# Attention with its VectorE queue reordered, the copy of O moved from ScalarE to VectorE, and V products two key tiles later

## What is computed

```python
x = x + attention(layernorm(x))
x = x + ffn(layernorm(x))
# attention, per sequence b and head h
q, k = rope(q), rope(k)                       # first 32 of 64 dimensions
sim  = einsum('bhid,bhjd->bhij', q, k) * 64 ** -0.5
attn = softmax(sim, axis=-1)
out  = einsum('bhij,bhjd->bhid', attn, v)     # heads joined, then @ Wout + bout
# ffn: gelu((x @ U1) @ V1 + b1) @ U2 @ V2 + b2
```

## Time and profile before

| | |
|---|---|
| median of 3 runs | 1569.16 us (1568.19 to 1571.64) |
| the profiled execution | 1572.87 us, its span 1570.9 us |
| PE busy | 1443.6 us, 92% of the span |
| ACT, POOL, DVE busy | 68%, 63%, 60% |
| chain that ended last | PE 73%, issue 8%, ACT 7%, POOL 5%, DVE 5% |

### The profile page before, as it was taken

One profiled execution on the slowest core, in us unless ns is written; L12 is line 12 of the kernel. 1 busy time (PEld: TensorE's weight loads), 2 busy tenths in 40 slices (PEclk: granted clock), 3 DMA queues, 4 the chain that ended last, 5 costly groups with the idle time before them and its releaser, 6 DMA issues.

```text
span 1570.9 us, 29110 instructions
## 1 busy us (share of the span) xinstructions
PE 1443.6 (92%) x7289; PEld 541.1 (34%) x7289; DVE 942.3 (60%) x1809; ACT 1063.3 (68%) x2024; POOL 988.6 (63%) x517
## 2 busy tenths in 40 slices
PE   3698999999999999999999999999999999998886
PEld 1133333333324333333424333332433333343323
DVE  7465665566565656656566566656665665657444
ACT  2476776677767677767767776767767676776564
POOL 4389856658485665748476575848566574848631
PEclk9699999999999999999999999999999999999999
DMA  5412131221303122220313122130312222031002
GB/s 149 86 31 54 33 80 23 57 58 38 77 14 79 27 60 51 56 59 14 79 36 75 27 57 58 26 80 24 79 23 59 56 52 63 14 79 37 1 15 67
DMA packets 76421, 80.76 MB, mean 51 GB/s; under 512 B 29252, under 2 KB 43080, under 8 KB 76072
## 3 DMA queue, kind: packets, MB, share of 16 engines
q1 hardware_dynamic: 74880, 78.89, 21.5%
q10 hardware_dynamic: 1448, 1.00, 0.3%
HBM read 22.56 MB, written 2.36 MB: 16 GB/s over the span
## 4 chain that ended last, share of the span: by engine, by line
PE 73%; issue 8%; ACT 7%; POOL 5%; DVE 5%; ACTq 1%; DMA 1%; SPq 0%; DVEq 0%; POOLq 0%
PE O L399 26%; PE S L387 13%; PE S L388 11%; PE MD L408 10%; PE TILE L319 4%; PE TILE L337 4%; PE TILE L313 3%; PE TILE L329 2%; ACT OS L504 2%; ACT PF L532 2%; ACT LEFT L517 2%; POOL SA L706 2%; DVE STAGE L556 1%; ACT STAGE L443 1%; POOL WRAW L299 1%
## 5 line engine op out<-in xcount | busy, mean ns | idle before, releaser
L706 POOL TENSOR_TENSOR SA<-PF 128x1024 f32<-128x1024 f32 x256 | 623.0, 2442 | 434.6 <-DVE SUM L633 292.2
L625 DVE CUSTOM_DVE_ANT_0 LEFT<-MR,LEFT 128x512 f32<-128x512 f32 x512 | 353.3, 690 | 481.8 <-ACT LEFT L517 477.1
L532 ACT ACTIVATE PF<-S 128x512 f32<-128x512 f32 x1024 | 553.1, 596 | 44.7 <-PE S L388 35.2
L517 ACT ACTIVATE LEFT<-MD 128x512 f32<-128x512 f32 x512 | 308.3, 602 | 381.8 <-PE MR L409 349.2
L399 PE MATMUL O<-PF,V 128*64 128x512 f32 x2048 | 502.7, 612 | 15.2 <-ACT OS L504 15.2
L387 PE MATMUL S<-QK 128*128 128x512 f16 x1024 | 393.2, 384 | 10.5 <-ACT PF L532 10.5
L388 PE MATMUL S<-QK 128*128 128x512 f16 x1024 | 389.2, 380 | 0.0
L408 PE MATMUL MD<-KD,QK 64*128 64x512 f16 x512 | 225.5, 440 | 15.8 <-ACT LEFT L517 9.1
L636 DVE TENSOR_TENSOR SUM<-SUM,SA 128x1024 f32<-128x1024 f32 x128 | 227.0, 1773 | 8.6 <-POOL SA L706 8.3
L409 PE MATMUL MR<-QK 64*128 64x512 f16 x512 | 225.8, 441 | 0.0
L399 PEld LDWEIGHTS O<-PF,V 128*64 128x64 f32 x2048 | 125.6, 137 | 225.4 <-issue 158.8
(11 more groups left out here) (101 smaller groups left out, 1001.3 us busy)
## 6 DMA issues: line engine op xcount, KB each, us to landing
QK<-STAGE SPq DMA_DIRECT2D x128, 256.0 KB, 3.2
QK<-STAGE SPq DMA_DIRECT2D x128, 128.0 KB, 3.1
RB<-den SPq DMA_DIRECT2D x128, 128.0 KB, 3.0
KD<-KDS SPq DMA_DIRECT2D x128, 32.0 KB, 2.7
X<-in_L_attn_queries SPq DMA_DIRECT2D x4, 512.0 KB, 12.9
RT<-DS SPq DMA_DIRECT2D x128, 2.0 KB, 1.7
out<-X SPq DMA_DIRECT2D x8, 256.0 KB, 2.3
WRAW<-in_L_attn_Wkv SPq DMA_DIRECT2D x1, 1024.0 KB, 8.9
```

The costliest lines, as they stand in the source:

```text
L517: e.activation(LEFT[:, side, :], MD[:, :], ACT.Relu).then_inc(left_over, 1)
L532: e.activation(PF[:, t % SLOTS, z * HALF:(z + 1) * HALF], S[:, bank_of(t, z), :], ACT.Exp, scale=EXP_SCALE).then_inc(exped, 1)
L625: e.tensor_tensor_reduce(LEFT[:, side, :], MR[side][:, :], LEFT[:, side, :], 1.0, LOWEST, ALU.add, ALU.max, MX[:, place % 2, q:q + 1]).the ...
L706: e.tensor_tensor(SA[:, (t // 2) % 2, :], PF[:, t % SLOTS, :], PF[:, t % SLOTS + 1, :], ALU.add).then_inc(two_summed, 1)
```

## The change

1. `dve_step` does the tile work of its own step: in odd steps before `dve_max`, in even steps behind it. Statistics, invert, sums and norm now stand behind both.
2. The copy of O goes from ACT (`kt` = 2) to DVE (`dve_copy_out`), first in the step `kt` = PV_LAG - 2 = 4.
3. `PV_LAG` is 6: V products come two steps later, a head's first at `kt` = 6.
4. Tiles move: q's second rot tile from step 11 to 12, its pass tile from 13 to 14, V tiles and output tiles of the earlier pair of heads two steps later, DOWN tiles of the last iteration too.
5. The 12 units ahead of the loop alternate between MD and S[2], and each waits for the last but one.

```diff
-PV_LAG = 4
+PV_LAG = 6
-QK_AT = (1, 3, 4, 7, 8, 10, 11, 13)
+QK_AT = (1, 3, 4, 7, 8, 10, 12, 14)
-V_AT = {14: (1, 0), 16: (1, 1), 22: (0, 0), 24: (0, 1)}
+V_AT = {16: (1, 0), 18: (1, 1), 22: (0, 0), 24: (0, 1)}
-OUT_AT = {17: (1, 0), 19: (1, 1), 28: (0, 0), 30: (0, 1)}
+OUT_AT = {19: (1, 0), 21: (1, 1), 28: (0, 0), 30: (0, 1)}
-DOWN_AT = (12, 18, 21, 22, 23, 24)
+DOWN_AT = (12, 14, 17, 23, 25, 26)
+        LESS = [MD[:, :], S[:, 2, :]]
 # act_step
-            if kt == 2 and (not it.first or h > 0):
-                act_copy_out(e, it.i * GH + h - 1, (h - 1) % GH)
 # dve_tiles
-            for n, kind, args in it.at(t - 1):
+            for n, kind, args in it.at(t):
+        def dve_copy_out(e, head, h):
+            rows = slice(DH * (h % 2), DH * (h % 2) + DH)
+            e.wait_ge(pv_done, KT * (head + 1))
+            wait(e, added, head - h % 2 - 2)
+            for z in range(2):
+                cp = e.tensor_copy(OS[rows, h // 2, z, :], O[DH * z:DH * z + DH, :])
+            cp.then_inc(o_copied, 1)
 # dve_step
-            dve_tiles(e, it, t)
+            if kt == PV_LAG - 2 and (not it.first or h > 0):
+                dve_copy_out(e, it.i * GH + h - 1, (h - 1) % GH)
+            if t % 2 == 1:
+                dve_tiles(e, it, t)
+            if not (it.last and u >= STEPS):
+                dve_max(e, it.step(u), it.i * GH + u // KT, (u // KT) % GH, u % KT, u % 2)
+            if t % 2 == 0:
+                dve_tiles(e, it, t)
             ... (statistics, invert, sums, norm as before)
-            if not (it.last and u >= STEPS):
-                dve_max(e, it.step(u), it.i * GH + u // KT, (u // KT) % GH, u % KT, u % 2)
 # ahead of the loop, PE (ACT likewise)
-                pe_unit(pe, u, u // KT, u % KT, u % 2)
+                wait(pe, left_over, u - 1)
+                pe_unit(pe, u, u // KT, u % KT, u % 2, LESS[u % 2])
 # behind the loop
-            act_copy_out(act, GROUPS * GH - 1, GH - 1)
+            dve_copy_out(dve, GROUPS * GH - 1, GH - 1)    # behind the last two dve_sum
```

More of the change, by code:

```diff
@@ L402, in pe_values, with pe_unit @@
             mm.then_inc(pv_done, 1)
-        def pe_unit(e, u, place, q, side):
-            wait(e, left_over, u)
+        def pe_unit(e, u, place, q, side, less):
             wait(e, max_read, u - 1)
-            e.matmul(MD[:, :], QHH[0:DH, place, q:N:KT], KD[:, place, :], start=True, stop=True)
+            e.matmul(less, QHH[0:DH, place, q:N:KT], KD[:, place, :], start=True, stop=True)
             e.matmul(MR[side][:, :], QHH[DH:P, place, q:N:KT], KMH[DH:P, place, 512:N],
@@ L416, in pe_next_unit @@
                 e.wait_ge(handed[place], HAND * (it.i + u // STEPS + 1))
-            pe_unit(e, it.step(u), place, q, u % 2)
+            e.wait_ge(left_over, it.step(u))
+            pe_unit(e, it.step(u), place, q, u % 2, MD[:, :])
         def pe_step(e, it, t):
@@ L496, in act_tiles @@
                     act_rot(e, args, it.i + 1)
[L498 to L505, removed]
         def act_max(e, head, place):
@@ L511, in act_max, with act_left @@
             e.activation(MN[:, place % 2, :], MX[:, place % 2, :], ACT.Copy, scale=-1.0 / MSCALE).then_inc(max_found, 1)
-        def act_left(e, u, side):
+        def act_left(e, u, side, less):
             e.wait_ge(unit_made, u + 1)
             wait(e, max_read, u - 1)
-            e.activation(LEFT[:, side, :], MD[:, :], ACT.Relu).then_inc(left_over, 1)
+            e.activation(LEFT[:, side, :], less, ACT.Relu).then_inc(left_over, 1)
         def act_step(e, it, t):
@@ L525, in act_step @@
             if t % 2 == 0 and more:
-                act_left(e, it.step(t + LEAD), t % 2)
+                act_left(e, it.step(t + LEAD), t % 2, MD[:, :])
             for z in range(2):
@@ L902, in _ @@
             for u in range(LEAD):
-                act_left(act, u, u % 2)
+                act_left(act, u, u % 2, LESS[u % 2])
                 if u == KT + 1:
```

## The result

The changed kernel takes **1605.07 us** (median of 4 runs, 1604.58 to 1607.7) against 1568.68 us for the kernel before on the same chip: a ratio of 1.0235 (1.0213 to 1.0258). It is 36 us slower. The forecast was 1582, slower by 13.

What follows compares the result with a forecast made beforehand. TensorE's work (92% of the span) plus its queue's gaps bounds the kernel. New gaps less 3.6 us make +1.3 an iteration, times 15 +19.5, less 2.4, 1.9 and 2.3: +13, so 1582 us; own range 1573 to 1600.

Steps and rivals of the forecast that it cites:

- copies of O at the other three heads: VectorE's copies end 2.2 to 3.3 us behind the V pair, TensorE wants O after 3.2 to 4.5: no gap.
- gap of step 15: TensorE's unit of step 16 waits for LEFT behind GpSimd's late rot_add: 1.1 us (0.6 to 1.6).
- last iteration: It makes no q and k and only sheds copies: 2.3 us saved.
- Step 1: Loses 0.95 us as ScalarE comes back late from the loop's end; nothing in the change alters that.
- Removed, 3.6 us an iteration: TensorE's gaps for O and tiles at steps 3, 4, 11 and 27, with small gaps, go: 3.6 us.
- chain from the sum to the unit of step 12: Sum at kt = 7 starts at +4.14, rot_add ends at +14.8, 3.3 us later; TensorE's gap at step 11 is 2.0 us.
- Copy of O at step 13: VectorE's copy follows maximum and sum; O is free at +19.8, wanted at +19.1: 0.6 us gap.
- Rival (c): Worse case, chance 0.06: stretched kt = 3 sums make copies late at steps 5 and 29, later gaps larger: 1613 us.
- The hand-over, 1.2: Transfers of q and k for the next iteration land at +40.2, TensorE wants them at +39.0: 1.2 us gap.
- The prologue, -2.4, and the tail, -1.9: Two banks save 2.4 us over the twelve units before the loop; last scores come 1.9 us earlier, gained at the tail.
- Rival (a): Faster case, chance 0.30: GpSimd not late; 1517 us with only the copy's 0.6 gap, 1547 with only step 11's.
- The lock: VectorE with two SBUF inputs and GpSimd exclude each other; copies of O out of PSUM cost GpSimd nothing, else up to 1.3 us.

Runs made afterwards that it cites:

- Run 1: The changed kernel with part 0 of the sum (kt = 7) first in its step on VectorE again, ahead of tile work and maximum: 1512.79 us.
- Run 12: The changed kernel with part 0 of the sum first, plus two idle 128x4 activations per head on ScalarE at kt = 2: 1528.46 us.
- Run 11: The changed kernel with part 0 of the sum first in the last iteration alone: 1604.24 us.
- run 4: The kernel before with only the prologue's twelve units alternating between two banks: 1567.91 us, ratio 0.9989.
- runs 9 and 10: The changed kernel with all three sums first on VectorE: 1539.19 us; with parts 0 and 2 first, part 1 behind the maximum: 1524.28 us.

## Why the prediction was wrong in size

The direction and the main mechanism held: the late sum drags GpSimd, and through it ScalarE's LEFT and the transfers. But +13 was forecast, and +32 measured between the profiled spans (+36 between medians, the profiled execution of before being 4 us over its median). The measured 1605 lies outside my own range of 1573 to 1600.

**The steps that failed.** Three terms of the sum. The copies of O at the other three heads were put at nothing: two of them cost 1.24 us an iteration. The gap of step 15 was put at 1.1 us: it measured 2.03. The last iteration was put at -2.3 us: it measured +2.8. Step 1, which was to stay, gave back 0.78 an iteration and hid part of this. Point by point:

- **Removed, 3.6 us an iteration: right.** Steps 3 and 4 gave 0.71, step 11 1.91, the old gaps of steps 13 and 14 0.25, step 27 0.74: 3.61 us. Step 17 gave 0.2 more.
- **The chain from the sum to the unit of step 12: right.** Forecast +4.14 for the sum, +5.4 for GpSimd's, +14.8 for the end of rot_add and 2.0 us of gap; measured +4.14, +5.43, +14.87, 2.03. Run 1, which moves the sum alone, shows the cause.
- **Copy of O at step 13, 0.6: came out at 0.17.** The copies took 1.38 (1.3 forecast); the sum ahead of them took 1.22, the low end of "1.2 us alone, up to 2". So TensorE was at the next unit 0.4 us earlier, which did not help.
- **Step 15, 1.1 us: mis-sized, 2.03.** The end of rot_add was +27.3, against "+26.2 to +27.2". VectorE's norm lay on GpSimd's sum and rot_add: the sum took 2.36 all the same, and T 2.27 in place of 1.26. The forecast had the norm nowhere in it; it had allowed up to 1.0 us, but for a stretched sum, and taken the middle. That is 0.5 to 0.6 of the miss; the other 0.4 is the missing delay of step 13. My own range stopped at 1.6.
- **"At the other three heads ... nothing": wrong, 0.65 at step 5 and 0.59 at step 29.** The copy stood behind a sum of 2.26 us (at 722.25), stretched by GpSimd's, and ended 3.7 us behind the V pair where TensorE wanted it at 3.2. I had said 2.2 to 3.3. Rival (c) named just this, at 0.3 to 0.6 each, and its 1613 is nearer to the measured 1605 than my 1582, but it got 0.06.
- **The hand-over, 1.2: measured 1.36 at step 19** (1.09 shown, the rest tile and modelled ends).
- **"Nothing in the change alters that", of step 1's 0.95: wrong, it fell by 0.78.** Run 12 shows that instructions less in ScalarE's program did it, not the copy's time on the path.
- An iteration is thus +2.3 in place of +1.3: 2.03 - 2.0 + 0.17 - 0.6 + 2.03 - 1.1 + 1.36 - 1.2 + 1.24 is 1.9 more, step 1 and step 17 are 1.0 less. Over 14 iterations that is 12.3 us of the miss of 19 (32 for 13); the first iteration, with 1.5 more than its share, and the last, with 5.1, make up the rest.
- **The last iteration, "only sheds copies, 2.3 us": +2.8, 5.1 us off, the most in any one iteration.** The late sum is in it too, and there it holds up GpSimd's row normalization for TensorE's tiles (idle 7.48 us, TensorE's gap 5.16). I looked at q and k only, which that iteration doesn't make. Run 11 puts 2.0 us of the loss down to this sum; the rest came with what the loop handed over, and its cause stays open.
- **The prologue, -2.4, and the tail, -1.9: right** (-2.24, which run 4 has alone, and -1.9).
- **Rival (a), the faster case, did not come**, but it was close in another sense: its price for a kernel without the gaps, 1517, is what run 1 measured within 5 us. In part this is luck: it had neither the 0.78 us of step 1 nor 1.06 at step 13 (0.6 there).
- **The lock.** GpSimd's sum at 747.28 took 3.35 us, 1.0 more than the 2.36 alone, with VectorE's sum (1.22, from 747.19) on it for 1.1 us; the copy of O (748.33 to 749.71) lay on the 2.3 us that remained. So the copy cost it nothing. By the Trainium skill (SBUF — State Buffer, section Who interferes with whom), VectorE reading two SBUF operands and GpSimd exclude each other and a copy out of PSUM doesn't; the trace agrees for the copy (no 1.3 us added) and for the norm (2.95 us, T 2.27).

## What to carry to other kernels

Before an instruction is put behind others in an in-order queue, follow who waits for its result to the end, in every form of the loop body, first and last too: the order moved one sum of 1.2 us by 3.3 us, which cost 92 us and turned a gain of some 56 into a loss of 36. When a change is good apart from one such place, as here (0.965 with the sum back, 1.0235 without), move the early producer alone and leave the others late. And when gaps go, ask what they covered: a later stage is then wanted earlier, as in runs 9 and 10.

## What the runs showed of the hardware that was not expected

**The loop's return.** ScalarE came back from the loop's end in about 2.48 us with nothing to wait for, in every kernel with the copies, or with two activations of 4 columns per head, in its loop (the page counts 2024 instructions of ScalarE, 2022 in run 12); with 1896 it was ready when TensorE's product came, after 1.55 us. TensorE's step 1 is 0.8 us shorter then. Whether it is the number of ScalarE's instructions or their place in memory that decides was not separated.

**TensorE's clock behind a gap.** Windows of 2 us (columns: length, busy times of PE, PEld, DVE, ACT and POOL with their instructions, the granted clock, the share of the transfers, GB/s). First the changed kernel's last iteration:

```profile
1463.00:1465.00 2.00, 2.00 (x7) 1.15 (x8) 0.37 (x1) 0.84 (x3) 2.00 (x2) 0.50 0.00 0
1465.00:1467.00 2.00, 2.00 (x6) 0.44 (x6) 1.10 (x5) 1.64 (x3) 1.92 (x3) 0.50 0.04 1
```

Behind its idle 3.57 us TensorE was granted half its clock, 1.2 of 2.4 GHz, for both windows, and ran the tile at 1462.88 in 1.09 us, where run 11 took 0.63 behind 2.02 us of idle time. The four matmuls of scores that followed stand 0.43 us apart instead of 0.22. So such a gap can cost more than its length.

It is not the gap's length alone that decides. At the gaps of 2.0 us of the loop iteration shown above the windows from 743 to 749 and from 757 to 763 have the full clock throughout. In the first two loop iterations of the same execution the clock fell behind the same gap of step 15, here behind the 1.98 us that end at 204.78:

```profile
206.00:208.00 2.00, 2.00 (x15) 1.52 (x14) 1.36 (x3) 1.19 (x3) 1.17 (x1) 0.50 0.00 0
```

These two iterations took 92.8 and 92.7 us. In the kernel before it is two of 14 as well, behind the 1.74 and 1.73 us of step 11, and they took 91.5 and 91.6 us against 89.85, which is most of the 4 us that this execution lies over its median:

```profile
282.00:284.00 2.00, 2.00 (x8) 0.33 (x4) 1.53 (x5) 0.00 (x0) 2.00 (x3) 0.50 0.00 0
462.00:464.00 2.00, 2.00 (x6) 0.61 (x8) 1.21 (x3) 0.60 (x1) 2.00 (x1) 0.50 0.00 0
```

Its last iteration has it twice, behind 3.06 and 2.32 us. What makes the clock fall behind one gap and not behind the next of the same length, no run here shows.
